# The last step of a two-iteration expert layer, cut into two column halves, on one core

## What is computed

```python
for _ in range(2):
    ctx = concat([integrated, v])
    # a shared network and the two experts chosen by a router, each:
    alpha, beta, gate = sigmoid(.), softplus(.), sigmoid(.)   # of gelu(ctx @ w1 + b1) @ w2 + b2
    v_next = alpha * v - beta * (x - mu)
    x_next = x + 0.1 * gate * v_next
    # x_next, v_next: weighted sums of the three (shared sw, experts (1 - sw) * p)
    halt = sigmoid(gelu(x_next @ w_h1 + b_h1) @ w_h2 + b_h2)
    refined = gelu(x_next @ w_f1 + b_f1) @ w_f2 + b_f2
    integrated = integrated + halt * refined * integration_weight
```

## Time and profile before

| | us |
|---|---|
| median of 3 runs | 370.67 |
| lowest, highest | 370.46, 371.39 |
| the profiled execution, its own time | 368.45 |
| its span (first to last instruction) | 366.7 |
| last DVE instruction ends | 364.0 |

### The profile page before, as it was taken

The page is one execution under the profiler, slowest core; times in us unless marked ns, Lnnn a source line. Parts: engine busy times, 40 slices in busy tenths (PEclk is TensorE's granted clock), DMA queues, the critical chain, the costliest instruction groups (busy, mean ns, idle before and its releaser), DMA issues.

```text
span 366.7 us, 4373 instructions
## 1 busy us (share of the span) xinstructions
PE 329.7 (90%) x1516; PEld 232.0 (63%) x1516; DVE 285.3 (78%) x596; ACT 196.7 (54%) x306; POOL 17.4 (5%) x20
## 2 busy tenths in 40 slices
PE   4989999898988777997998999999999999998952
PEld 4754886455555555575775776777777777776630
DVE  0556766646867778989999999999998997993952
ACT  2500034485555473396767765866468456538522
POOL 0040011211110102000000000000000000000000
PEclk9989999999999999599999999999999999999988
DMA  7999910000000000000000000000000000000000
GB/s 261 426 414 290 347 70 0 1 1 2 0 0 3 0 0 2 0 2 1 1 2 0 0 0 2 0 2 1 0 1 2 0 0 30 0 0 30 0 29 29
DMA packets 10726, 17.85 MB, mean 49 GB/s; under 512 B 337, under 2 KB 8529, under 8 KB 9425
## 3 DMA queue, kind: packets, MB, share of 16 engines
q1 hardware_dynamic: 10704, 17.58, 13.8%
HBM read 16.53 MB, written 1.05 MB: 48 GB/s over the span
## 4 chain that ended last, share of the span: by engine, by line
PE 55%; DVE 25%; issue 11%; ACT 4%; POOL 2%; DMA 2%; POOLq 1%; ACTq 0%; DVEq 0%; SPq 0%
PE ps L1124 50%; DVE zz L761 3%; DVE lst L746 2%; POOL lrs L347 2%; PE ps L1221 2%; DMA ctxT<-in_ctxT 2%; DVE kv L1048 1%; DVE ring L855 1%; DVE kv L1049 1%; DVE kv L1047 1%; DVE kv L1051 1%; PE ps L1200 1%; DVE st L646 1%; DVE lmv L749 1%; DVE ctxT L1077 1%
## 5 line engine op out<-in xcount | busy, mean ns | idle before, releaser
L1124 PE MATMUL ps<-hm_odd,ew_hi 128*128 128x512 f32 (+1 forms) x169 | 52.8, 417 | 0.0
L1124 PE MATMUL ps<-hm_even,ew_hi 128*128 128x512 f32 (+1 forms) x160 | 49.7, 414 | 0.0
L1124 PEld LDWEIGHTS ps<-hm_odd,ew_hi 128*128 128x128 f32 (+1 forms) x169 | 29.6, 189 | 6.4 <-issue 0.2
L1124 PEld LDWEIGHTS ps<-hm_even,ew_hi 128*128 128x128 f32 (+1 forms) x160 | 27.5, 188 | 5.2
L1124 PE MATMUL ps<-hm_odd,ew_lo 128*128 128x512 f32 (+1 forms) x80 | 28.6, 395 | 0.0
L1124 PE MATMUL ps<-hm_even,ew_lo 128*128 128x512 f32 (+1 forms) x80 | 28.0, 389 | 0.0
L467 ACT ACTIVATE hid<-ps,pB 128x512 f32<-128x512 f32 x32 | 21.8, 688 | 10.4 <-PE ps L1124 9.8
L1124 PE MATMUL ps<-x_hi,w1x_hi 128*128 128x512 f32 x40 | 19.8, 495 | 4.2 <-ACT hid L467 3.9
L761 DVE TENSOR_SCALAR zz<-ps,lmv,lrs 128x128 f32<-128x128 f32 x48 | 16.4, 404 | 7.7 <-POOL lrs L347 7.5
L855 DVE SCALAR_TENSOR_TENSOR ring<-ring,pB,hid 128x1024 f32<-128x1024 bf16 x16 | 20.5, 1282 | 0.9
L746 DVE BATCH_NORM_STATS2 lst<-ps 128x6 f32<-128x128 f32 x48 | 10.7, 285 | 11.9 <-PE ps L1200 11.8
(11 more groups left out here) (272 smaller groups left out, 749.3 us busy)
## 6 DMA issues: line engine op xcount, KB each, us to landing
ring<-in_fc1b SPq DMA_DIRECT2D x4, 1024.0 KB, 17.4
ring<-in_fc2a SPq DMA_DIRECT2D x4, 1024.0 KB, 8.4
packC<-in_packC SPq DMA_DIRECT2D x1, 1152.0 KB, 9.4
pB<-in_packB SPq DMA_DIRECT2D x1, 1125.5 KB, 9.9
ctxT<-in_ctxT SPq DMA_DIRECT2D x2, 512.0 KB, 6.5
xtok<-in_xtok SPq DMA_DIRECT2D x1, 1024.0 KB, 9.1
xT<-in_xT SPq DMA_DIRECT2D x1, 1024.0 KB, 11.1
a<-in_fc1a SPq DMA_DIRECT2D x1, 1024.0 KB, 13.1
```

Source lines behind the costliest of these rows:

```text
L1124: return pe.matmul(out, lhsT, rhs, start=start, stop=stop)
```

## The change

- Two products with weights move ahead of the squashes. `last_factors` (DVE) makes `last_w` from v, `ne`, `cb` and `swc`: four instructions, queued behind state_next_split(6) and ahead of halt_low(6). It lies where `hm_even` lay, which the GATE products of step 6 read, and waits for these. `stepped(7)` is then three instructions of 3 x 512 columns; the weighting by `cb` and by `swc` is gone.
- refine_b(6) on PE goes behind GATE(7); refine2(6) on ACT goes behind `last_gate`; refine(6) on DVE goes behind `last_stepped`. The 9 unread products become 4.
- From the third slice of GATE(7) on, everything is done in two halves of HC = 256 columns: its tanh, `xn`, the refinement, the halt, the output and its transfer (two of 128 KB).
- Step 7's refinement multiplies plain float32 operands (`W("wf1")`, `wh1f`, `W("wh2")`), so `xn` and h1 are not split: three DVE instructions and one ACT instruction go, and ten float32r and two plain products of 512 columns (14 records) become twelve plain ones of 256 columns (24 records). `wh1f` adds 32 columns to pB, and `wf1_lo` moves into pA so that wf1 stays whole.

```diff
@@ -32,7 +32,7 @@
 VB = CH // VK
 VG = -(-B // VB)
 PACK_B = [("ew1", 128, 2 * E * H), ("ws1", 128, 4 * H), ("wq", 128, D),
-          ("wf1", 128, 2 * D), ("wh1", 128, 4 * 32), ("bq", 128, 1), 
+          ("wf1", 128, 2 * D), ("wh1", 128, 4 * 32), ("wh1f", 128, 32), ("bq", 128, 1), 
...
+        last_w = nc.alloc_sbuf_tensor_at("last_w", [128, 6 * CH], F, offset=hm_even_at)[:, :]\
+            .rearrange("p (a k n) -> p a k n", a=2, k=3)
...
-        wf1_lo = placed("wf1_lo", 2 * D, pB_at + 4 * colB["wf1"][1])
+        wf1_lo = placed("wf1_lo", 2 * D, pA_at + 4 * (nA - 2 * D))
...
+        HC = CH // 2
+
+        def cut(i):
+
+            return slice(i * HC, (i + 1) * HC)
...
-            for c in range(NCH):
+            for c in range(NCH - 1):
 
                 sp.wait_ge(sem("res"), c + 1)
                 sp.dma_start(d_out[:, ck(c)], res[:, ck(c)]).then_inc(sem("out"), 16)
-            sp.wait_ge(sem("out"), 16 * NCH)
+            for i in range(2):
+                part = slice((NCH - 1) * CH + i * HC, (NCH - 1) * CH + (i + 1) * HC)
+                sp.wait_ge(sem("res"), NCH + i)
+                sp.dma_start(d_out[:, part], res[:, part]).then_inc(sem("out"), 16)
+            sp.wait_ge(sem("out"), 16 * (NCH + 1))
...
             def last_gate():
 
                 n = group_of(STEPS - 1, GATE)
-                for k in range(3):
+                for k in range(2):
                     act.wait_ge(sem("stream_ps"), k + 1)
                     act.activation(bg[:, 1, k], group_ps(n)[:, k, :], ACT.Tanh, scale=0.5,
                                    bias=0.0 if k else bs2h[:, GATE:GATE + 1]).then_inc(sem("stream"), 1)
+                act.wait_ge(sem("stream_ps"), 3)
+                for i in range(2):
+                    act.activation(bg[:, 1, 2, cut(i)], group_ps(n)[:, 2, cut(i)], ACT.Tanh, scale=0.5)\
+                        .then_inc(sem("stream"), 1)
+
+            def last_hidden(i):
+
+                act.wait_ge(sem("lf_ps"), 3 * i + 1)
+                if i == 0:
+                    act.wait_ge(sem("h2_ps"), STEPS - 1)
+                act.activation(h1[0:32, cut(i)], bank[3 * i][0:32, 0:HC], ACT.Gelu, bias=W("bh1")[0:32])\
+                    .then_inc(sem("lfh"), 1)
+                for j in range(2):
+                    act.wait_ge(sem("lf_ps"), 3 * i + j + 2)
+                    act.activation(fh[:, j, cut(i)], bank[3 * i + j + 1][:, 0:HC], ACT.Gelu,
+                                   bias=W("bf1", j, j + 1)).then_inc(sem("lfh"), 1)
+
+            def last_halt(i):
+
+                act.wait_ge(sem("lh2_ps"), i + 1)
+                if i == 0:
+                    act.wait_ge(sem("res"), NCH - 1)
+                act.activation(th[:, cut(i)], bank[1 + i][:, 0:HC], ACT.Tanh, bias=bh2h[:, 0:1], scale=0.5)\
+                    .then_inc(sem("lth"), 1)
 
...
                     squashed(s, GATE)
+            last_gate()
             refine2(STEPS - 2)
-            last_gate()
-            refine1(STEPS - 1)
-            halt1(STEPS - 1)
-            refine2(STEPS - 1)
+            for i in range(2):
+                last_hidden(i)
+            for i in range(2):
+                last_halt(i)
...
+            def last_factors():
+
+                s, c = STEPS - 1, NCH - 1
+                v = vT[:, ck(c)]
+
+                def twice(a):
+                    return a.unsqueeze(1).to_broadcast([128, 2, CH])
+
+                dve.wait_ge(sem("part_ps"), group(s - 1, 2) + 1)
+                link(dve.scalar_tensor_tensor(last_w[:, 0, 1:3], cb[:, c], 0.5, twice(v), ALU.mult, ALU.mult))
+                link(dve.tensor_scalar(last_w[:, 0, 0], v, swc[:, 2:3], 0.5, ALU.mult, ALU.mult))
+                dve.wait_ge(sem("ne"), s + 1)
+                link(dve.tensor_tensor(last_w[:, 1, 1:3], cb[:, c], twice(ne), ALU.mult))
+                link(dve.tensor_scalar(last_w[:, 1, 0], ne, swc[:, 2:3], None, ALU.mult))
+
...
+                if s == STEPS - 1:
+                    dve.wait_ge(sem("squash"), 2 * group_of(s, BETA) + 2)
+                    link(dve.tensor_tensor(bg[:, 0], bg[:, 0], last_w[:, 1], ALU.mult))
+                    dve.wait_ge(sem("squash"), 2 * group_of(s, ALPHA) + 2)
+                    link(dve.scalar_tensor_tensor(al, al, 1.0, last_w[:, 0], ALU.add, ALU.mult))
+                    link(dve.tensor_tensor(al, al, bg[:, 0], ALU.add))
+                    return
...
-                    if s == STEPS - 1:
-                        return
...
-                for k in range(3):
+                for k in range(2):
                     dve.wait_ge(sem("stream"), k + 1)
-                    dve.scalar_tensor_tensor(g[:, k], g[:, k], 1.0, al[:, k], ALU.add, ALU.mult)\
-                        .then_inc(sem("gated"), 1)
-                    dve.wait_ge(sem("gated"), k + 1)
-                    if k == 1:
-                        link(dve.scalar_tensor_tensor(g[:, 0], g[:, 0], swc[:, 2:3], g[:, 1], ALU.mult, ALU.add))
-                        link(dve.scalar_tensor_tensor(g[:, 0], g[:, 0], 0.05, x, ALU.mult, ALU.add))
+                    link(dve.scalar_tensor_tensor(g[:, k], g[:, k], 1.0, al[:, k], ALU.add, ALU.mult))
+                    link(dve.scalar_tensor_tensor(g[:, 0], g[:, k], 0.05, g[:, 0] if k else x, ALU.mult, ALU.add))
                 dve.wait_ge(sem("h1_ps"), s)
-                dve.scalar_tensor_tensor(xn, g[:, 2], 0.05, g[:, 0], ALU.mult, ALU.add).then_inc(sem("xn"), 1)
+                for i in range(2):
+                    dve.wait_ge(sem("stream"), 3 + i)
+                    link(dve.scalar_tensor_tensor(g[:, 2, cut(i)], g[:, 2, cut(i)], 1.0, al[:, 2, cut(i)],
+                                                  ALU.add, ALU.mult))
+                    dve.scalar_tensor_tensor(xn[:, cut(i)], g[:, 2, cut(i)], 0.05, g[:, 0, cut(i)],
+                                             ALU.mult, ALU.add).then_inc(sem("xn"), 1)
+
+            def last_refine():
+
+                c = (NCH - 1) * CH
+                for i in range(2):
+                    dve.wait_ge(sem("lth"), i + 1)
+                    link(dve.tensor_scalar(th[:, cut(i)], th[:, cut(i)], 1.0, iwh[:, 0:1], ALU.add, ALU.mult))
+                for i in range(2):
+                    out = slice(c + i * HC, c + (i + 1) * HC)
+                    dve.wait_ge(sem("lf2_ps"), i + 1)
+                    link(dve.scalar_tensor_tensor(rr[:, cut(i)], bank[3 * i][:, 0:HC], W("bf2"), th[:, cut(i)],
+                                                  ALU.add, ALU.mult))
+                    dve.tensor_tensor(res[:, out], xT[:, out], rr[:, cut(i)], ALU.add).then_inc(sem("res"), 1)
...
+                if s == STEPS - 1:
+                    last_factors()
                 if s >= 1:
                     halt_low(s - 1)
                 if s == 0:
                     slot_masks(NCH - 1)
             stepped(STEPS - 1)
+            last_stepped()
             refine(STEPS - 2)
-            last_stepped()
-            state_next_split(STEPS - 1)
-            halt_low(STEPS - 1)
-            refine(STEPS - 1)
+            last_refine()
...
-                if s == STEPS - 1:
-                    refine_b(s - 1)
                 if s >= NCH:
                     controls(s, GATE)
+            refine_b(STEPS - 2)
             pe.wait_ge(sem("squash"), 2 * LAST)
-            for k in range(9):
+            for k in range(4):
                 mm(bank[0], ew2_hi[:, 0:D], masked(STEPS - 1)[:, 0, 1, :])
-            refine_a(STEPS - 1)
-            halt_a(STEPS - 1)
-            refine_b(STEPS - 1)
+            for i in range(2):
+                pe.wait_ge(sem("xn"), STEPS + i)
+                for k, w in enumerate((W("wh1f"), W("wf1", 0, 128), W("wf1", 128, 256))):
+                    out = bank[3 * i + k]
+                    mm(out[0:32, 0:HC] if k == 0 else out[:, 0:HC], w, xn[:, cut(i)]).then_inc(sem("lf_ps"), 1)
+            for i in range(2):
+                pe.wait_ge(sem("lfh"), 4 if i else 2)
+                mm(bank[1 + i][:, 0:HC], W("wh2")[0:32].to_broadcast([32, 128]), h1[0:32, cut(i)])\
+                    .then_inc(sem("lh2_ps"), 1)
+            for i in range(2):
+                pe.wait_ge(sem("lfh"), 3 * i + 3)
+                for j in range(2):
+                    last = mm(bank[3 * i][:, 0:HC], W("wf2", j * 128, (j + 1) * 128), fh[:, j, cut(i)],
+                              start=j == 0, stop=j == 1)
+                last.then_inc(sem("lf2_ps"), 1)
```

More of the change, by code:

```diff
@@ L1616 @@
         wr1=x("w_r1"), br1=col(x("b_r1"), 32), wr2=np.concatenate([x("w_r2"), x("b_r2")[None]], 0),
-        wh1=np.tile(x("w_h1"), (1, 4)), bh1=np.tile(col(x("b_h1"), 32), (4, 1)),
+        wh1=np.tile(x("w_h1"), (1, 4)), wh1f=x("w_h1"), bh1=np.tile(col(x("b_h1"), 32), (4, 1)),
         wh2=np.concatenate([x("w_h2")] * 3 + [np.zeros((32, 1), f32)], 0), bh2=rep(x("b_h2")),
```

## The result

| | before | changed kernel |
|---|---|---|
| median, us | 370.56 | 360.50 |
| lowest, highest | 370.15, 371.39 | 360.22, 361.15 |
| ratio, 95% interval | | 0.9727, 0.971 to 0.9743 |
| profiled execution, its own time | 368.45 | 360.35 |
| its span | 366.7 | 358.6 |

The change saves 10.06 us by the medians, where 9.0 was forecast; the time (360.495, the middle of 360.35 and 360.64) lies at the lower edge of the range (360.5), by the third decimal outside it. But the two profiled executions are only 8.1 apart, less than 9.0. So two things are to be explained: why the profiles give 0.9 less than forecast, and why the medians give 2.0 more than the profiles. Two errors of opposite sign hid each other in part; that the time came out so near the range is luck to that extent.

A forecast was written before the change was run, and what follows sets the result against it. From 338.87 DVE bounds the last step, then a PE, ACT, DVE chain, then the transfer. DVE's end at 355.4 plus 2.3 gives 357.7, 9.0 below 366.7; off the median 370.67: 361.7, range 360.5 to 364.3.

The forecast's parts named there:

- the ladder up to xn: Last step: DVE, last to arrive, ends the xn halves at 348.84 and 349.77; PE starts at 348.94, 4.34 earlier.
- Factors and order: DVE ahead of xn: last_factors fits the idle 6.11 us, a 1.22 product goes, refine(6)'s two of 0.69 move behind xn.
- a pitch of 0.217 and 0.434 per product: 348.94 + 12 x 0.434: PE behind xn: twelve plain 256-column products, two records each, reach 354.15, the last ending at 354.31; DVE ends at 355.4.
- Halving: Last stretch in two 256-column halves: worth 1.4 us against an unsplit end at 359.1.
- the transfer: Output at the end: 128 KB instead of 256 KB takes 0.4 less, 2.3 us instead of 2.70 (bounds 2.3 and 2.7).
- I subtract 9.0 from the median: Whole time: the 9.0 us saved on the profiled execution's stamps, taken off the median of 370.67, gives 361.7.
- rival 3: Last step: timed runs before lacked the profile's low clock, so only about 7.8 can be won: 362.9; chance 0.1.
- 1 (halves bring nothing): Last stretch: second halves do not overlap, through fixed parts and extra semaphore waits: 363.1; chance 0.08.
- 2 (GATE waits for ALPHA): PE in step 7: GATE starts near 341.4, not earlier, so products start 1.5 later: 363.2; chance 0.08.
- 4 (low clock on the twelve products): PE behind xn: all twelve at half speed cost 5.2 more, 366.9; half of them, 364.3; chance 0.1.
- 5 (slower): DVE: last_factors delays halt_low(6) past 338.87; slower than before if its instructions end after 347.9; chance 0.02.
- Table sets: the hidden batching unit: ACT's gelu and tanh switches: forecast no table load; if the skill's rule held, about 1.1 more, 362.8.

The follow-up runs named there:

- a_same: Changed kernel with all twelve plain products in one 128 x 128 stationary form (first halt weights in four copies, second zero-padded): median 359.69 us, ratio 0.9715 to the kernel before.
- b_hot: Kernel before with 22 unread products instead of 9 ahead of xn and 8 more between halt_a and refine_b of step 7: median 368.06 us, ratio 0.9931.
- a_full: Changed kernel with the last stretch in one piece of 512 columns instead of two halves, one output transfer of 256 KB: median 362.08 us.
- plain_only: Kernel before with only step 7's refinement changed to plain products at full width; factors, order, 9 unread products, one transfer as before: median 364.08 us, ratio 0.9851.
- a_onedma: Changed kernel with one output transfer of 256 KB behind the second half instead of two of 128 KB: median 361.00 us.

## Why the prediction was right and wrong

**Right: the ladder up to xn.** Every stamp of that part is met within 0.2 us: `last_factors` done at 336.31 (337.0 at the latest), the h1s remainder at 339.03 behind 2.72 idle, GATE at 339.65 (339.5), the first half tanh at 345.64 (345.46), unread products done at 348.48 (348.54), the halves of `xn` at 348.91 and 349.70 (348.84 and 349.77). DVE was the last to arrive, as the sum had it. Factors and order, at 1.38 and 1.33 in the experiments, are what the rows gave, 1.3 and 1.4.

**Wrong by a term: "a pitch of 0.217 and 0.434 per product: 348.94 + 12 x 0.434".** The pitch of a record is right inside a form. At each of five changes of form 0.16 to 0.18 more goes by: from the start of the first record to that of the last it is 5.90 instead of 23 x 0.217 = 5.0, and a_same, without the changes, has 5.07. The row I took it from has one form only, so it could not show this. PE started at 348.96 (348.94 forecast) and ended at 355.23 instead of 354.31, and DVE's end came as much later, at 356.28 instead of 355.4. These 0.9 us are what the profiles give less than forecast. Halving was put at 1.4 and is worth 0.74 and 0.36 for the transfer, 1.1.

**Right: the transfer**, 2.32 for 2.3, and 2.68 with one transfer of 256 KB.

**Wrong: "I subtract 9.0 from the median".** The sum was made against the profiled execution, whose time of 368.45 I saw to be 2.2 below the median, and I moved the difference over unchanged. That holds only if the 2.2 lie outside the stretch that the change shortens, and they do not: of the 2.85 between the two profiled executions of the kernel before (368.45 and 371.30), 2.29 lie in S. In the first, low clock left the last plain products at 1.95; in the second they take 3.75. The profile of the changed kernel has no low clock in S. Against the second execution it gains 27.42 - 17.25 = 10.2 in S, 0.33 in the transfer and 0.40 by an earlier front, 10.9 in all; that execution is 0.74 longer than the median of 370.56, from which 10.06 is counted.

**Wrong: the sign in rival 3.** It had low clock as the thing that could differ between profiled and timed runs, and its place, but went only one way: timed runs with less of it. That the profile was below all timed runs then at hand (370.46 the lowest) spoke for the other way, and I did not weigh it. Its size was read high too: my rows gave 3.70 - 2.3 = 1.4 on PE, of which the sum used 1.2, and against b_hot it is 0.99 in S.

Of the rivals: 1 (halves bring nothing) fell, a_full. 2 (GATE waits for ALPHA) fell, GATE starts at 339.65 while ALPHA's squash ends at 341.43; the releaser named in the earlier trace rows was not the cause. 4 (low clock on the twelve products) did not occur in the profile, and the times of the other executions, 361.15 at most, leave no room for half of it, 2.6 us. 5 (slower) fell with 2.72 us of idle time to spare. ACT goes from tanh to gelu at 349.62 and back at 352.92 with no load between, and loads are as many as before at each of their lines. The Trainium skill, "ScalarE: Activation LUTs", "Table sets: the hidden batching unit", lists gelu in another set than tanh; this trace, like that of the kernel before, contradicts it. Halves do cost a second fixed part, 0.42 for 256 columns where half of 0.69 is 0.35, but the overlap gains more. The Trainium skill, "VectorE: DVE Perf Modes", "The TRN2 errata", has SBUF operands pay a fixed latency for each instruction, and the trace agrees.

What the 10.06 us consist of, by S and the span: plain products 3.45, factors 1.38, order 1.33, halves 0.74, transfer 0.36, together 7.3; and low clock, 2.5 by the medians against b_hot, which makes 9.8. With the 3.28 of the second profile in place of the 2.5 it would be 10.5. The 10.06 lie between, and the difference is within the scatter of the front, whose own cause stays open. One thing goes with it in the fourteen profiles: three (the first of the kernel before, plain_only, a_onedma) have 10.5 us of low clock near 144 to 156 and none at 174 to 180, and their S starts at 338.49 to 338.87; the other eleven have 7.0 us near 146 to 156 and 3.4 at 174 to 180, and their S starts at 338.91 to 339.90. No experiment was made on it.

## What to carry to other kernels

Before a sum made on a profile is taken off a median, ask why the two differ, and whether the difference lies in the stretch that the change touches; a profiled execution that is faster than every timed one may belong to a rarer kind of execution. Where an engine's last stretch is a ladder of short dependent pieces, its waits can cost more than their length, through the clock of what follows: filling two of them with unread products (b_hot) took 2.5 us off the median, though no work was removed. A wait is no sure sign of it, as plain_only's of 2.17 us brought no low clock. And small products in a row were cheaper here in one form, padded, than each in its own.

## What was not expected of the hardware

- The same program falls into two groups of times, 367.8 to 369.2 and 369.7 to 371.8, with mean clocks of 0.969 to 0.974 and 0.958 to 0.964. In the two profiled executions the difference lies in the last 15 us: low clock came during or just behind a wait of PE of 3.4 us and stayed, at 1.2 GHz, for 16.8 us to the end in one and for 3.4 us in the other, with the same instruction order.
- A plain float32 record of 256 columns follows the one before at 0.217 while the stationary operand keeps its form; a change between 32 and 128 columns or rows costs 0.16 to 0.18 (6.27 us with five changes, 5.45 with none).
- A one-source DVE instruction on float32 in SBUF takes 0.49 at 512 columns with a scalar operand read from memory and 0.35 at 256, against 0.69 and 0.42 for two sources.
